# Two interleaved streams of transformer steps on one core: the hand-kept lists that merge them are written anew

## What is computed

```python
x = x + _L0_xattn_ref(_layernorm(x), ctx_512, ...)   # 16 heads of width 8: causal self plus cross attention
x = x + _L0_ffn_ref(_layernorm(x), ...)              # router, top 2 of 8 experts, 128 -> 512 -> 128
x = x + _L1_xattn_ref(_layernorm(x), ctx_512, ctx_512, ...)   # one head of width 128
x = x + _L1_ffn_ref(_layernorm(x), ...)              # 16 heads of width 64, gated values, top-2 output gates
```

```python
q = jnp.einsum('btc,hdc->bhtd', x, Wq); k = jnp.einsum('btc,hdc->bhtd', x, Wk)
w, sel = jax.lax.top_k(gate_v, K)
v = jnp.einsum('bthe,bted->bhtd', mix_v, proj_v)
probs = jax.nn.softmax(jnp.einsum('bhid,bhjd->bhij', q * scale, k), axis=-1)
attn = jnp.einsum('bhij,bhjd->bihd', probs, v)
res = jnp.einsum('bthe,bthd,efd->bthf', mask_o, attn, Wo)
```

## Time and profile before

| | |
|---|---|
| device time, three runs | 1278.98, 1280.1, 1280.35 us (median 1280.1) |
| profiled execution | 1274.52 us, its span 1272.8 us |
| mean granted PE clock | 0.855 of full speed |
| busy | PE 1118.9 us (88%), PEld 874.8 (69%), DVE 700.1 (55%), ACT 491.0 (39%), POOL 82.8 (7%) |
| chain that ended last | PE 74%, DVE 12%, ACT 7%, issue 2%, SP queue 2%, DMA 2% |

### The profile page before, as it was taken

One profiled execution on the slowest core, in us unless ns is written; L12 is line 12 of the kernel. 1 busy time (PEld: TensorE's weight loads), 2 busy tenths in 40 slices (PEclk: granted clock), 3 DMA queues, 4 the chain that ended last, 5 costly groups with the idle time before them and its releaser, 6 DMA issues.

```text
span 1272.8 us, 21333 instructions
## 1 busy us (share of the span) xinstructions
PE 1118.9 (88%) x8499; PEld 874.8 (69%) x8499; DVE 700.1 (55%) x1867; ACT 491.0 (39%) x1022; POOL 82.8 (7%) x246
## 2 busy tenths in 40 slices
PE   5888879899989998999989988998989998984696
PEld 4547645787569765887578855986678766873475
DVE  5503474856576565746575666657475657515400
ACT  4233406352434525352534434462536253422120
POOL 0020001000100001000100011000100010000000
PEclk8557958899889979898889978998889988998556
DMA  8000001051301421042103321052105220143322
GB/s 220 1 1 5 1 1 36 5 81 42 68 5 30 71 55 41 11 74 68 40 5 62 48 68 19 13 80 63 36 5 83 58 48 1 31 78 80 56 44 54
DMA packets 198033, 56.86 MB, mean 45 GB/s; under 512 B 173568, under 2 KB 193838, under 8 KB 197934
## 3 DMA queue, kind: packets, MB, share of 16 engines
q1 hardware_dynamic: 195630, 51.20, 20.6%
q10 hardware_dynamic: 2304, 4.29, 1.1%
HBM read 31.36 MB, written 24.12 MB: 44 GB/s over the span
## 4 chain that ended last, share of the span: by engine, by line
PE 74%; DVE 12%; ACT 7%; issue 2%; SPq 2%; DMA 2%; ACTq 0%; DVEq 0%
PE bank L737 10%; PE bank L928 10%; PE bank L773 9%; PE bank L843 5%; PE bank L884 5%; PE bank L663 4%; PE bank L624 3%; PE bank L678 3%; DVE negmax L1265 3%; PE bank L911 3%; ACT pa L1022 2%; PE bank L588 2%; PE bank L942 2%; ACT hi_part L1008 2%; PE bank L832 2%
## 5 line engine op out<-in xcount | busy, mean ns | idle before, releaser
L1265 DVE TENSOR_REDUCE negmax<-bank 128x2 f32<-128x512 f32 (+1 forms) x224 | 139.0, 683 | 57.2 <-PE bank L624 35.0
L1022 ACT ACTIVATE pa<-bank 128x512 f32<-128x512 f32 x224 | 123.4, 596 | 111.6 <-PE bank L678 73.7
L1039 ACT ACTIVATE pa<-bank,b_c 128x256 f32<-128x256 f32 x256 | 107.5, 471 | 117.9 <-PE bank L737 115.8
L737 PE MATMUL bank<-xnT_a,w 128*128 128x256 f32 x512 | 141.8, 429 | 0.1
L928 PEld LDWEIGHTS bank<-vb,pb 128*128 128x128 f32 x1024 | 129.6, 209 | 7.8 <-ACT pb L1101 3.0
L928 PE MATMUL bank<-vb,pb 128*128 128x65 f32 x1024 | 133.8, 294 | 1.2 <-ACT pb L1101 0.8
L773 PE MATMUL bank<-w,pa 128*128 128x128 f32 x1024 | 124.2, 276 | 0.0
L773 PEld LDWEIGHTS bank<-w,pa 128*128 128x128 f32 x1024 | 121.9, 192 | 3.2
L737 PEld LDWEIGHTS bank<-xnT_a,w 128*128 128x128 f32 x512 | 107.0, 219 | 18.4 <-ACT pa L1039 0.7
L1101 ACT ACTIVATE pb<-bank 128x512 f32<-128x512 f32 x128 | 69.8, 599 | 111.8 <-PE bank L888 110.9
L1419 DVE TENSOR_REDUCE negc<-bank 128x2 f32<-128x512 f32 x128 | 80.0, 684 | 46.4 <-PE bank L860 46.1
(11 more groups left out here) (239 smaller groups left out, 1690.5 us busy)
## 6 DMA issues: line engine op xcount, KB each, us to landing
v_d<-at SPq DMA_DIRECT2D x32, 256.0 KB, 3.3
vb<-v_d SPq DMA_DIRECT2D x32, 256.0 KB, 5.3
at_d<-at SPq DMA_DIRECT2D x32, 256.0 KB, 2.1
at<-at_d SPq DMA_DIRECT2D x32, 256.0 KB, 4.4
pv_d<-pvs SPq DMA_DIRECT2D x8, 512.0 KB, 2.8
pvs<-pv_d SPq DMA_DIRECT2D x16, 256.0 KB, 4.2
w<-in_L_ffn_W_dram ACTq DMA_DIRECT2D x1, 2048.0 KB, 10.5
bd<-mix_d SPq DMA_DIRECT2D x128, 8.0 KB
```

What stands on the lines that cost most here:

```text
L737: mm = pe.matmul(BA[u % 2][:, c * T:(c + 1) * T], w1[:, e, f:f + P], xnT_a[:, :], start=True, stop=True)
L1022: nc.scalar.activation(pa[:, e % NPA, :], BA[e % 2][:, :], ACT.Exp, scale=SC0).then_inc(S["a_ex"], 1)
L1039: ins = nc.scalar.activation(hT[:, u % 4, c, :], BA[u % 2][:, c * T:(c + 1) * T], ACT.Relu, bias=b1_c[:, k:k + 1])
L1265: nc.vector.tensor_reduce(negmax[:, i:i + ng], BA[j][:, :].rearrange("p (g k) -> p g k", g=ng), AX, ALU.max, negate=True).then_inc(S["a_mx ...
```

## The change

The change replaces the four lists and two tuples of numbers. No step is added, removed or written differently; only their order in the merged program differs. One line is added, so that lines below L380 count one more in the changed kernel.

```diff
--- before.py
+++ after.py
@@ -353,30 +353,31 @@
 
         STEPS_A = [("a_values", 0), *run("a_max", 0, 7), ("a_shift", 0), *run("a_score", 0, 14), ("a_lastpv", 0),
                    ("a_heads", 0), ("a_project", 0), ("a_norm2", 0), ("c_kv", 0), ("a_norm2_apply", 0),
-                   ("a_router", 0), ("a_expert", 0), ("a_expert", 1), ("f_load", 0), *run("a_expert", 2, 6),
-                   ("f_norm", 0), ("a_expert", 6), ("a_expert", 7), ("f_norm_apply", 0), ("a_last", 0),
-                   ("c_norm", 0), ("f_stack", 0), ("c_norm_apply", 0), ("f_stack", 1), ("c_q", 0), ("f_stack", 2),
-                   ("c_max", 0), ("f_stack", 3), ("f_stack", 4), ("c_turn", 0), ("f_stack", 5), ("c_out", 0),
-                   ("f_stack", 6), ("f_stack", 7)]
-        STEPS_B = [("b_norm", 0), ("b_norm_apply", 0), ("b_gates", 0), ("b_top2", 0), *run("b_split", 0, 8),
-                   *run("b_max", 0, 4), ("b_top2", 1), *run("b_max", 4, 8), ("b_top2", 2), ("b_shift", 0),
-                   ("b_fill", 0), ("b_mix", 0), ("b_score", 0), ("b_mix", 1), ("b_score", 1), ("b_sel", 0),
-                   ("b_score", 2), ("b_score", 3), ("b_attend", 0), ("b_score", 4), ("b_score", 5),
-                   ("b_attend", 1), ("b_score", 6), ("b_score", 7), ("b_attend", 2), ("b_attend", 3),
-                   ("b_weigh", 0), ("b_gather", 0), ("b_gather", 1), ("b_out", 0)]
-        AFTER_A = (67, 67, 68, 68, 70, 71, 74, 75, 76, 77, 78, 78, 79, 80, 84, 84, 85, 88, 88, 89, 89, 90, 93, 95,
-                   96, 99, 99, 100, 105, 107, 110, 111, 111, 112, 113, 114, 114, 115, 116, 116, 119, 119, 120)
+                   ("a_router", 0), *run("a_expert", 0, 5), ("f_load", 0), ("f_norm", 0),
+                   ("a_expert", 5), ("a_expert", 6), ("f_norm_apply", 0), ("a_expert", 7), ("a_last", 0),
+                   ("f_stack", 0), ("c_norm", 0), ("f_stack", 1), ("f_stack", 2), ("c_norm_apply", 0),
+                   ("f_stack", 3), ("c_q", 0), ("c_max", 0), ("f_stack", 4), ("c_turn", 0), ("f_stack", 5),
+                   ("c_out", 0), ("f_stack", 6), ("f_stack", 7)]
+        STEPS_B = [("b_norm", 0), ("b_norm_apply", 0), ("b_gates", 0), ("b_top2", 0),
+                   ("b_split", 0), ("b_split", 1), ("b_top2", 1), *run("b_split", 2, 8), *run("b_max", 0, 3),
+                   ("b_top2", 2), ("b_fill", 0), *run("b_max", 3, 8), ("b_shift", 0), ("b_mix", 0), ("b_score", 0),
+                   ("b_mix", 1), ("b_score", 1), ("b_sel", 0), ("b_score", 2), ("b_score", 3), ("b_attend", 0),
+                   ("b_score", 4), ("b_score", 5), ("b_attend", 1), ("b_score", 6), ("b_score", 7),
+                   ("b_attend", 2), ("b_attend", 3), ("b_gather", 0), ("b_gather", 1), ("b_weigh", 0),
+                   ("b_out", 0)]
+        AFTER_A = (64, 70, 71, 72, 72, 74, 74, 75, 75, 77, 78, 78, 80, 84, 84, 85, 85, 85, 85, 86, 87, 89, 89, 93,
+                   99, 101, 101, 104, 104, 108, 112, 113, 114, 114, 115, 116, 117, 118, 119, 123, 124, 125, 125)
         assert len(AFTER_A) == len(STEPS_B)
 
-        LAST_B = [("b_norm", 0), ("b_norm_apply", 0), ("b_gates", 0), ("b_top2", 0), *run("b_split", 0, 3),
-                   ("b_top2", 1), ("b_top2", 2), *run("b_split", 3, 8), ("b_max", 0), ("b_fill", 0),
-                   *run("b_max", 1, 4), ("b_sel", 0), ("b_mix", 0), ("b_mix", 1), *run("b_max", 4, 8),
-                   ("b_shift", 0), *run("b_score", 0, 4), ("b_attend", 0), ("b_score", 4), ("b_score", 5),
-                   ("b_attend", 1), ("b_score", 6), ("b_score", 7), ("b_attend", 2), ("b_attend", 3),
+        LAST_B = [("b_norm", 0), ("b_norm_apply", 0), ("b_gates", 0), ("b_top2", 0), *run("b_split", 0, 5),
+                   ("b_top2", 1), *run("b_split", 5, 8), ("b_top2", 2), *run("b_max", 0, 3), ("b_fill", 0),
+                   ("b_max", 3), ("b_mix", 0), ("b_mix", 1), ("b_sel", 0), *run("b_max", 4, 8), ("b_shift", 0),
+                   *run("b_score", 0, 4), ("b_attend", 0), ("b_score", 4), ("b_score", 5), ("b_attend", 1),
+                   ("b_score", 6), ("b_score", 7), ("b_attend", 2), ("b_attend", 3),
                    ("b_gather", 0), ("b_gather", 1), ("b_weigh", 0), ("b_out", 0)]
-        LAST_AFTER = (62, 66, 67, 70, 70, 73, 81, 86, 90, 90, 90, 90, 90, 90, 90, 90, 90, 90, 95, 111, 111, 112,
-                   113, 119, 121, 125, 129, 130, 130, 130, 130, 130, 130, 130, 130, 130, 135, 135, 135, 135, 135,
-                   135, 140)
+        LAST_AFTER = (65, 71, 76, 76, 81, 81, 81, 84, 92, 92, 98, 99, 99, 99, 99, 99, 99, 101, 121, 135, 137, 147,
+                   147, 147, 149, 149, 149, 149, 149, 149, 149, 149, 149, 149, 149, 149, 149, 149, 149, 149, 149,
+                   154, 161)
         assert len(LAST_AFTER) == len(LAST_B)
 
         def stream_b(q):
```

## The result

The change takes 1283.29 us (median of 20 runs, 1281.06 to 1286.45), the kernel before 1277.55 us on the same chip (20 runs, 1273.48 to 1283.13). The ratio is 1.0047, with a 95% interval of 1.0035 to 1.0058: **slower by about 6 us**, where 1290 was forecast against 1280.1. The forecast's sign holds and the number lies just inside its range, but the parts of the sum are wrong in both directions, so that this is luck. The profiled execution took 1286.45 us, the slowest of the 20, with a span of 1284.7; that is 11.9 more than the profiled one before, whose 1274.52 us lie near the lowest of the 20. What follows takes the 11.9 apart, and a typical pair of executions differs by half of it. Where a kernel has runs over 1.5% above its fastest (only the sixth experiment has, two of them), its ratio leaves them out.

The account below looks back on a forecast made before the run. PE was taken as the bound, busy 129.98 of 139.9 us. Six rounds +6.3, first round +2.0, last sequence +2.8 and a covered wait -0.9 sum to +10.2 on 1280.1, giving 1290; own range 1283 to 1303, whole range 1270 to 1310.

Parts of the forecast that it names:

- The waits of a round: In each full round, waits gained at the maxima and lost elsewhere sum to +1.6 us.
- The wait at the turn: Behind the turn of the maxima, PE waits for DVE ahead of the first a_score, as b_out no longer fills in: +1.6 us.
- that for xn_b: Ahead of xn_b's transposes in stream B's norm, PE waits for DVE's copy, xn_b and signalling: +1.2 us a round.
- the 2.6 that the sum takes off for the maxima: Scores and an attend between the later steps of maxima cut lost time from 4.6 to 2.05 us a round.
- The gates' clock: b_gates' two projections leave the low clock and run at 1.13 and 1.88 us: 2.15 us back a round.
- What follows at half speed: Behind the turn's wait: gather slow as before, two scores +0.5, values +0.9, b_out +0.9; together +2.3 us a round.
- First round: Stream B's first round: three scores now follow one another and wait for ACT, +2.0 us.
- In stream A's last third attention a `b_score` now covers a wait ahead of `c_max`: -0.9: At the end, one score step fills a PE wait in stream A's last third attention, giving 0.9 us back.
- the low clock reaches the attends: Clock falls inside the fifth step of maxima; two attends take 7.09 us, some 7 us a round hit: 1311, chance 0.14.
- Last sequence: Five more DVE splits ahead of the mixing weights delay b_mix(0): 2.8 us; all behind only shifts, already in the low clock.
- The low clock goes: The wait behind the turn is too short to lower the clock, so the gather runs at full speed: 1272, chance 0.30.
- Only waits count: Only long idle gaps lower the clock, so rounds cost their waits alone: sum +13.5, 1294 us, chance 0.08.

Follow-up runs that it names:

- sixth experiment: The change with added 128x512 matmuls into an unread bank, seven ahead of a_score(0), two each ahead of a_score(1) and (2): 1267.41 us, ratio 0.994.
- second experiment: The kernel before with only the last sequence's new lists, all rounds by the old lists: 1284.36 us, ratio 1.0056.
- fourth experiment: The change with nine 128x512 matmuls into an unread bank ahead of the wait of sequence 6's first attend: 1269.18 us, ratio 0.9937.
- ninth: The change with five positions of sequence 6's stream B moved by one to three places, as in the kernel before: 1266.68 us, ratio 0.9916.
- fifth experiment: The kernel before with the last sequence's new lists, but its b_norm at position 64 instead of 65: 1280.07 us, ratio 1.0033.
- 3: The change with the last pass in which both streams are full, and the last sequence, by the old lists: 1264.77 us, ratio 0.9908.
- 8: The kernel before with added matmuls in the waits of its end, none ahead of sequence 6's first attend: 1281.22 us, ratio 1.0039.
- 12: The ninth's kernel with sixteen 128x512 matmuls into an unread bank, once, ahead of the last sequence's first attend: 1253.55 us, ratio 0.9815.
- experiment 1: The change with the last sequence's own lists put back, all rounds by the new lists: 1279.97 us, ratio 1.0019.

## Why the prediction was right or wrong

**The waits of a round: right in the main.** The wait at the turn is 1.61 (forecast 1.6) and that for xn_b 1.06 (1.2). `c_turn` grew by 0.45, not 1.0: the `f_stack` that is left and the steps of stream B beside it cover more than I counted. Ahead of `a_heads` a wait of 0.6 appeared (forecast 0.1). PE's idle time grew by 11.54 - 9.92 = 1.6 us, the same number as the forecast's sum, but by chance: of the 2.6 that the sum takes off for the maxima, most was busy time of matmuls that came singly, not idle time.

**The gates' clock: right.** 1.13 and 1.88 us, as forecast; 2.15 us a round.

**"What follows at half speed: ... two scores, +0.5; one set of values ...; and `b_out`": the step that failed in the rounds.** The clock does fall behind the wait of 1.6 us, as forecast, but it is back at 747.5, after scores and gather alone. Values (1.07) and `b_out` (2.06) ran at the full clock, so 1.8 of the +2.3 us a round were not there; the scores' part was (1.28, 1.28 and 0.79 us for three of them). The low stretches around maxima and gates sum to 13.6 us in the earlier trace rows and 10.2 now; I had let one stretch cover seven steps in a row, which none of the rows showed. Nor was the clock full up to the turn, as I had it: it dipped once, at 723.6. The round came to -3.4 instead of +1.05. Of the 2.65 us that are left of this difference, 0.55 are `c_turn` and 0.3 the maxima (in the grouped lines of a round their two lines of scores have 8.2 us busy and idle before and 5.3 now, 2.9 where 2.6 were forecast). The same lines have 0.5 us less busy time for the experts' first matmuls (18.0 to 17.5), 0.4 less for the splits and 0.3 less for the `f_stack` steps; the rest I cannot assign. `b_out`'s price in the low clock was mis-sized too: 3.79, so +1.7 and not +0.9 (the sixth experiment and the end show it).

**First round:** +4.8 instead of +2.0, mis-sized. Kernels with the old rounds differ here by themselves: the router of sequence 2 stands at 372.35 us in the kernel before and at 375.18 in the second experiment. In the changed kernel this round has a low stretch of 46 us (164.9 to 211.1), before one of 37 (164.6 to 201.6), so a part is clock, which the forecast had not counted here; how much was not separated.

**"In stream A's last third attention a `b_score` now covers a wait ahead of `c_max`: -0.9": the step that failed at the end.** The wait ahead of `c_max` is gone, but one of 1.06 us now stands ahead of `c_q` (1101.43) where there was none, as the same `b_score` had covered it. From the transposes of `c_norm` to the first attend the two kernels take the same time, 12.36 us before and 12.29 now, so the 0.9 was not there. And I followed the five steps of stream B for the waits only, not for the clock. Before, it dipped ahead of the attends, `c_out` took 2.07 us, and 0.75 us of wait for `vb` was left. Now it does not dip, `c_out` takes 1.16, the wait is 1.90, and behind it all four attends lose the clock. That cost 16.1 us in the attends and scores and 4.4 in `b_out` and gates in the traced execution. The fourth experiment gives back 14 us by filling that wait alone, the ninth 17 by moving those five steps. The mechanism was named, as the rival in which "the low clock reaches the attends", at 7.09 us each and with a wait in the maxima as its cause; I had looked for it in the steady rounds, where it never came (3.69 to 3.79 us), and given it 0.14.

**Last sequence:** 2.8 us forecast for the longer way to the mixing weights; some 2.6 in the fifth experiment's trace. In the change itself `b_mix(0)` starts 29.3 us after the gates, before 25.0; 2.6 of these 4.3 us lie between the gates and the splits, at the low clock now. The last `b_out`'s 1.7 us came on top: "All behind it is in the low clock already" was wrong for it, since before it ran at 2.06.

**The rivals.** "The low clock goes" (1272) is nearest for the rounds alone, by their time though not by its reason, as the gather stayed slow. "Only waits count" rested on the Trainium skill, TensorE: Matmul & The Clock Gate, HAM oscillation, which has long idle gaps of TensorE bring the clock down. I read it as the only cause, which the rest of the page does not claim. The trace agrees for long gaps: in the kernel before the clock fell at 1150.0, within the 7.34 us that the gather waits. It shows falls at short ones too: the clock fell for 61 us behind a wait of 1.90 us, and filling that wait took 14 us off.

So the forecast was near the measured time by luck: it had 24 us too much in the rounds, 23 too little at the end and 3 too little in the first round. These are errors against the traced pair, 11.9 us apart; the medians are 5.7 apart.

## What to carry to other kernels

A merged order has to be read where it is not periodic, in the first and the last pass, with the question of which wait stands directly ahead of the longest run of work that did not lift the clock by itself in the trace: 1.90 us of wait there cost 16. Moving the dip to a cheaper place, or filling the wait with a few matmuls of 512 columns into an unread bank, can be worth more than the order's own gain. The filling must fit inside the wait, since ahead of a chain of DMAs it only delays them.

## What was not expected of the hardware

The same attends with the same scores ran through 61 us at 1.2 GHz (PE busy 49.7 of 61.4 us) and through 27 us at 2.4 GHz, by the level at which they began; sixteen 128x512 matmuls changed the level. Where nothing was filled in ahead of sequence 6's attends, they ran at 3.8 us in each trace in which the clock had dipped shortly before them (the kernel before, experiments 2, 3, 5, 6, 8, 9 and 12) and at 6.6 to 7.1 in the two in which it had not (the change, experiment 1). Why a dip goes with this is not shown. And the same kernel can spread: 16 us over the eight runs of the sixth experiment up to 1278.4 (clock 0.854 to 0.867), against 1.3 us over the four of the fourth.
